# One PSUM eviction moved from VectorE to ScalarE, and eight one-column adds made one, in a two-block transformer kernel

## What is computed

```python
x = x + 0.5 * ffn(layernorm(x), w_up, w_down)
x = x + attn(layernorm(x), guidance)          # guidance: 512 x 1024
x = x + 0.5 * ffn(layernorm(x), w_up, w_down)

# ffn: ternary-quantized w_up (4096 x 1024) and w_down (1024 x 4096),
#      rms-normalised input, gelu between the two
# attn: diffs d[t] = x[t+1] - x[t], normalised to unit length;
#       softmax over 2 * cosine(d[t], guidance) picks a mix of guidance rows;
#       0.6 * d + 0.4 * mix, weighted by tanh(2 |d|) and a position ramp,
#       summed over a window of the 8 earlier diffs, divided by the weights' sum
```

## Time and profile before

| | us |
|---|---|
| median of 3 timed runs | 7212.81 |
| lowest and highest of them | 7123.75, 7471.04 |
| the profiled execution | 7010.74 |
| its span on the slowest core (core 1) | 7009.2 |
| spans of the eight cores | 6945.0 to 7009.2 |
| TensorE matmuls busy | 5356.2 (76%) |
| VectorE busy | 1494.8 (21%) |
| ScalarE busy | 1644.0 (23%) |

### The profile page before, as it was taken

The page is one execution under the profiler, slowest core; times in us unless marked ns, Lnnn a source line. Parts: engine busy times, 40 slices in busy tenths (PEclk is TensorE's granted clock), DMA queues, the critical chain, the costliest instruction groups (busy, mean ns, idle before and its releaser), DMA issues.

```text
span 7009.2 us, 63588 instructions; the slowest of 8 cores (6945.0 to 7009.2 us)
## 1 busy us (share of the span) xinstructions
PE 5356.2 (76%) x22802; PEld 2603.7 (37%) x22802; DVE 1494.8 (21%) x3961; ACT 1644.0 (23%) x2980; POOL 21.5 (0%) x57
## 2 busy tenths in 40 slices
PE   1158788788878878787887878787788878778778
PEld 0123333334333333433333333333333333333333
DVE  4641111211121121112112111211212121121221
ACT  3442212122222212122221212222121222212112
POOL 0000000000000000000000000000000000000000
PEclk9998789889989888898988989899898989989889
DMA  6520000000000000000000000000000000000000
GB/s 195 153 61 1 1 7 7 6 7 1 13 1 7 7 7 7 1 13 1 7 7 7 7 0 13 1 7 7 6 7 1 13 1 7 7 7 7 1 6 7
DMA packets 67124, 106.85 MB, mean 15 GB/s; under 512 B 7424, under 2 KB 42240, under 8 KB 66816
## 3 DMA queue, kind: packets, MB, share of 16 engines
q1 hardware_dynamic: 62208, 86.01, 4.2%
q0 software_dynamic: 4608, 16.78, 0.6%
HBM read 85.98 MB, written 16.78 MB: 15 GB/s over the span
## 4 chain that ended last, share of the span: by engine, by line
PE 73%; DVE 10%; ACT 7%; issue 6%; DMA 2%; SPq 1%; DVEq 0%; ACTq 0%; POOL 0%; POOLq 0%
PE PT_A L643 28%; PE PT_C L659 8%; PE PT_G L659 7%; PE PT_E L659 7%; PE PT_F L659 7%; PE PT_C L808 4%; PE PT_B L845 4%; PE PT_B L593 3%; DVE gfm_h L605 3%; ACT BIGf L628 2%; PE PT_E L759 2%; PE PT_C L720 2%; PE PT_B L731 1%; DVE xr L694 1%; DMA astgD<-wdn 1%
## 5 line engine op out<-in xcount | busy, mean ns | idle before, releaser
L643 PE MATMUL PT_A<-wqdnT,gfm_h 128*128 128x512 bf16 x4096 | 1007.6, 403 | 286.0 <-DVE gfm_h L605 286.0
L643 PE MATMUL PT_A<-wqdnT,gfm_l 128*128 128x512 bf16 x4096 | 935.5, 382 | 38.2
L610 DVE TENSOR_TENSOR gfm_l<-PT_B,gfm_h 128x512 bf16<-128x512 f32 x512 | 354.3, 692 | 2147.3 <-ACT gfm_h L600 1220.3
L643 PEld LDWEIGHTS PT_A<-wqdnT,gfm_h 128*128 128x128 bf16 x4096 | 411.6, 102 | 828.0 <-issue 440.0
L593 PE MATMUL PT_B<-identf,BIGf 128*128 128x128 f32 x2560 | 378.5, 297 | 350.4 <-ACT BIGf L585 341.4
L628 ACT ACTIVATE BIGf<-BIGf 128x1024 f32<-128x1024 f32 x256 | 270.0, 1055 | 1489.3 <-PE PT_A L643 1489.3
L643 PEld LDWEIGHTS PT_A<-wqdnT,gfm_l 128*128 128x128 bf16 x4096 | 384.5, 98 | 589.2 <-issue 188.6
L593 PEld LDWEIGHTS PT_B<-identf,BIGf 128*128 128x128 f32 x2560 | 331.3, 154 | 423.5 <-issue 375.4
L605 DVE CAST gfm_h<-PT_B 128x512 bf16<-128x512 f32 x256 | 177.1, 692 | 1356.6 <-ACT BIGf L628 1343.1
L659 PE MATMUL PT_C<-wqupT,xnT_h 128*128 128x512 bf16 x1024 | 314.8, 463 | 43.0 <-ACT xnT_h L600 33.4
L808 PE MATMUL PT_C<-gsT,BIGf 128*128 128x512 f32 x512 | 305.7, 764 | 0.0
(11 more groups left out here) (191 smaller groups left out, 4251.6 us busy)
## 6 DMA issues: line engine op xcount, KB each, us to landing
xr<-x SPq DMA_DIRECT2D x32, 512.0 KB, 3.7
astgU<-wup SPq DMA_DIRECT2D x64, 256.0 KB, 4.1
BIGf<-wup SPq DMA_DIRECT2D x128, 128.0 KB, 3.4
astgD<-wdn SPq DMA_DIRECT2D x64, 256.0 KB, 4.9
BIGf<-wdn SPq DMA_DIRECT2D x128, 128.0 KB, 2.6
out<-xr POOLq DMA_DIRECT2D x32, 512.0 KB, 2.9
guidN<-guid SPq DMA_DIRECT2D x16, 128.0 KB, 3.4
```

The lines of the kernel that those rows point to most:

```text
L610: vop(lambda e, dst_h=dst_h, dst_l=dst_l, half=half: e.tensor_sub(dst_l[:, half * 512:(half + 1) * 512], PT_B[:, half * 512:(half + 1) * 512],
L643: e.matmul(PT_A[:, nh * 512:(nh + 1) * 512], src[:, i * 128:(i + 1) * 128], wqdnT[:, fg * D + nh * 512: fg * D + (nh + 1) * 512], start=(q ...
```

## The change

The eviction of PT_B to BS[3] in `attn_front_pe` goes from VectorE's queue (`vop`, `tensor_copy`) to ScalarE's (`sop`, `copy`). In `attn_back`, the eight adds of one column each become one add over a strided view of BS[3] with 8 elements in each partition, 128 elements apart; in the last chunk, the eight memsets become one in the same way. All else stays.

```diff
@@ -733,26 +733,21 @@
-        vop(lambda e: e.tensor_copy(BS[3], PT_B),
+        sop(lambda e: e.copy(BS[3], PT_B),
             reads=[bF["PT_Blo"], bF["PT_Bhi"]], writes=[bF["S3"]])
 
     def attn_back(c):
         xa = xr[c % 4]
         xbuf = bX[c % 4]
+        d127 = BS[3].rearrange("p (j t) -> p j t", j=8)[:, :, 127:128]
         if c + 1 < nch:
-            ln2c1 = ln2c1r[(c + 1) % 4]
+            ln2c1 = ln2c1r[(c + 1) % 4].rearrange("p (j o) -> p j o", o=1)
             lb = bF[f"ln2c1_{(c + 1) % 4}"]
-            for dj in range(8):
-                vop(lambda e, dj=dj, ln2c1=ln2c1: e.tensor_add(
-                    BS[3][:, dj * 128 + 127: dj * 128 + 128],
-                    BS[3][:, dj * 128 + 127: dj * 128 + 128],
-                    ln2c1[:, dj:dj + 1]),
-                    reads=[lb], writes=[bF["S3"]])
+            vop(lambda e, d127=d127, ln2c1=ln2c1: e.tensor_add(
+                d127, d127, ln2c1), reads=[lb], writes=[bF["S3"]])
         else:
-            for dj in range(8):
-                vop(lambda e, dj=dj: e.memset(
-                    BS[3][:, dj * 128 + 127: dj * 128 + 128], 0.0),
-                    writes=[bF["S3"]])
+            vop(lambda e, d127=d127: e.memset(d127, 0.0),
+                writes=[bF["S3"]])
         sop(lambda e: e.activation(BS[2], BS[3], AF.Square),
             reads=[bF["S3"]], writes=[bF["S2"], bF["gfm_h"], bF["gfm_l"]])
```

## The result

Each kernel was run 22 times, and as in many runs the cores of one die go at a lower granted clock, only the runs without that are compared, and not the medians over all of them (7236.23 us, and 7071.34 for before). The changed kernel takes 0.9914 of the time of the one before, with a 95% interval of 0.9874 to 0.9954: it is 0.5 to 1.3% faster. For figures of a few microseconds this document uses the spans of undisturbed dies: the median of the four cores of a die, taken over the dies that lie within 0.4% of that kernel's lowest. This is 6944 us for before (28 dies, 6929 to 6956) and 6901 us for the changed kernel (25 dies, 6892 to 6913), 43 us or 0.62% less. The experiments ran on three chips, and on each of them the dies of before have their median at 6943 or 6944 us. The forecast was 33 us, or 0.47%, and a time of 7179.

A forecast was written before the change was run, and what follows sets the result against it. TensorE carries 73% of the chain and idles in the tails during the edited lines. Even tails 29.3 plus odd tails 3.7 gave 33.0 us off 7010.7 profiled, 0.47%, so 7179 us timed from 7212.8; range 7070 to 7300.

The forecast's parts named there:

- even tail: End of even chunks, TensorE idle before L759: merging the adds gains 1.83 us each, 29.3 us over 16 chunks.
- strided add: L746 in the tails: one 128x8 add takes 0.17 us, where eight dependent adds took 2.00 us.
- even front: Front of even chunks: ScalarE's eviction is hidden by 2.8 us of cover before table load and first Gelu; cost 0.
- odd tail: End of odd chunks: merged add frees at most 0.68 us, the move eats 0.45; gain 0.23 each, 3.7 us in all.
- L585 took over as its bound: Odd tail: with one add, L756 is held by L585, the Identity ahead of it in ScalarE's queue.
- That gives 1690.35, 0.45 later than now: Odd tail: L546 starts at 1690.35 because L538 waits behind ScalarE's eviction, 0.45 us later than before.
- The clock's term: L808 after the tails: an earlier start may run slow or raise the clock earlier; 24 us either way, taken as 0.
- rival 2: Even chunks: clock rises earlier and L808 gets as short as in odd ones; 57 us gained, 7154 timed; chance 0.15.
- The argument against rival 2: L808: the odd chunk has a shorter idle stretch before it, as L731 runs there.
- within 2%: Whole kernel: a change within 144 us, which a measurement can't tell from no change; chance 0.94.
- rival 3: Odd chunk: ScalarE's copy causes two more table loads ahead of L538; 8 us slower, 7221 timed; chance 0.08 including other odd-chunk losses.

The follow-up runs named there:

- run 22: Not a label of a single run: the words say that each kernel, before and changed, was run 22 times; ratio 0.9914.
- odd_both: Against the kernel before: eviction on ScalarE in all chunks, one merged add in odd chunks, eight adds kept in even ones; undisturbed dies 6884 us against 6944.
- four_adds: Against the kernel before: four two-column adds instead of eight in even chunks, eviction left on VectorE; undisturbed dies 6901 us (three dies) against 6944.
- the pair with filler: Kernel before and changed kernel, each with unused matmuls in the idle stretches of both tails; 6923 us (2 dies) and 6936 us (8 dies).
- the order: Against before: adds merged, eviction on VectorE, square and norms moved earlier in both tails, similarities also in even ones; 6631 us (9 dies), 313 less.

## Why the prediction was right and wrong

**Right in place and sign of each step.** The even tail gained 1.84 us (forecast 1.83). The strided add cost 165 ns (170), which bounds for this case the penalty of the page "SBUF — State Buffer" of the Trainium skill (section on the DMA port swizzle): with eight elements at a 512-byte step, nothing of it is seen. The even front hid the move. The odd tail paid for the move in ScalarE's queue and L585 took over as its bound. No table load came; by the rule of the Trainium skill that copy is in every set ("ScalarE: Activation LUTs", section on table sets) there should be none, and the 64 and 64 loads agree.

**The odd tail was sized too small.** "That gives 1690.35, 0.45 later than now" was 0.29. The copy took 1.01 instead of 1.05, and L538 started 0.91 after the copy did, not 1.05: two ScalarE instructions in a row overlap by 0.10, and the same happened between L585 and the square. So the gain was 0.49 in this tail instead of 0.23. The sum's term of 3.7 us for the odd tails was 9.2, the even tails' 29.3 was 29.9, and together 39 us of idle went away where the sum had 33.

**The clock's term was taken as 0, with bounds of 24.** For this change it came out near that, a rest of 4 us on the side of the gain. Rival 2 gives 57 us, and the timed ratio of 0.9914 (61 us of 7071) looks like it, but the undisturbed dies say 43, and the ratio's interval holds both. The value was lucky rather than right. The argument against rival 2, a shorter idle stretch in the odd chunk, was thin too: right ahead of the norms TensorE waits 7.7 us there against 3.48 in the even tail. The clock's share moves at other places all over the pair of chunks, not only in L808, and odd_both has 51 us from it by itself, more than twice my bound, with four_adds at 25. I priced the clock at the one place that is edited, and should have priced it over all stretches behind an idle TensorE.

**The step that failed is the verdict.** The text set "within 2%" as what can't be told from no change and put 0.94 on it, as if an effect of half a percent couldn't be found. With 22 runs of each the interval is 0.8% wide, and 0.5 to 1.3% faster is clear of it. The mechanisms of the forecast all but one ended on the faster side (from 57 us less to nothing), and only rival 3 with 0.08 on the slower, so the text should have said faster, by half a percent to one. The time of 7179 and its range rested on the median of three runs, which varies by more than the change. That the changed kernel's median, 7236.23, falls into the range of 7070 to 7300 is luck: of its 22 runs 6 do. In the sum itself the mis-sized term is the odd tails'. Against the undisturbed dies the sum, 33 us, is 10 short of 43: 6 from the tails, nearly all of it the odd ones, and 4 from the clock.

What is open: which stretch gets the upper clock level in which kernel. The lower level's time accounts for the rests to within 10 us on average over cores, but nothing run here predicts it from the edit, and the pair with filler, where the path's gain should have come out alone, has the changed kernel slower.

## What to carry to other kernels

A chain of small operations that TensorE waits for took its own length off the idle time, or added it, in every kernel here but the pair with filler, and one strided add (0.17 us) did the work of eight dependent one-column ones (0.26 each). The span follows that only to within tens of microseconds. Moving an eviction from VectorE (21% busy) to ScalarE (23%) gained nothing that shows, as neither engine is the bound, and it costs what stands behind it in the new queue. Look at what the idle stretch waits for by its place in the queue, not only by its data: here the order was worth seven times the edit. And where the granted clock changes level many times, price an edit with tens of microseconds of clock either way, and judge it on undisturbed dies.

## What the hardware showed that I had not expected

- The time at the lower clock level is not local. Shortening 16 odd tails by 0.57 us each (odd_both) took some 108 us off it over the undisturbed dies (mean clock 0.913 against 0.906), and the feed-forward's matmuls, as many as before, ran 43.5 us faster in three groups on the two cores compared.
- The effect doesn't look monotone: from eight dependent operations to four, two and one the undisturbed dies stand at 6944, 6901, 6922 and 6908 us, the second on three dies only.
- Back-to-back ScalarE instructions overlap by 0.10 us (the copy from 1621.45, 1.01 long, and the next at 1622.36).
